# First attention with content and spatial head halves in three packed projections, with its last two blocks and the next stage's first gates in a new order

## What is computed

```python
q = (x @ Wq + bq) ...   # 2 heads of 64 features; k the same
q_content, q_spatial = (q[..., :half], q[..., half:])      # half = 32
q_spatial = _nrope(q_spatial...)                           # x1*cos - x2*sin, x1*sin + x2*cos
q = jnp.concatenate([q_content, q_spatial], axis=-1)       # k the same
score = jnp.einsum('bhqd,bhkd->bhqk', q, k) / sqrt(64)
attn = softmax(score); out = einsum('bhqk,bhkd->bhqd', attn, v)
return out.transpose(...).reshape(B, T, E) @ Wo + bo
```

## Time and profile before

| | |
|---|---|
| median of 3 runs | 709.2 us (709.16 to 710.09) |
| profiled execution, its own time | 709.26 us |
| span of the profiled execution | 707.5 us |
| mean granted clock of TensorE | 0.986 |
| first attention | from 0 to about 139 us of the span |
| busy over the span | TensorE 92%, VectorE 70%, ScalarE 64%, GpSimd 60% |

### The profile page before, as it was taken

One profiled execution on the slowest core, in us unless ns is written; L12 is line 12 of the kernel. 1 busy time (PEld: TensorE's weight loads), 2 busy tenths in 40 slices (PEclk: granted clock), 3 DMA queues, 4 the chain that ended last, 5 costly groups with the idle time before them and its releaser, 6 DMA issues.

```text
span 707.5 us, 14026 instructions
## 1 busy us (share of the span) xinstructions
PE 652.9 (92%) x4713; PEld 455.8 (64%) x4716; DVE 498.2 (70%) x958; ACT 450.7 (64%) x801; POOL 425.5 (60%) x443
## 2 busy tenths in 40 slices
PE   3789998799999999997999999998989999999997
PEld 1455555477777877675555555555546777787785
DVE  6879998676556778466778888877678565776521
ACT  3678886546665566545676677776765565666664
POOL 4545543368778777533346645654666877778673
PEclk9999999899999999998999999999999999999999
DMA  6101230000000000560467666664221000000001
GB/s 197 41 22 42 54 42 1 1 0 2 1 0 0 0 1 1 188 229 3 138 198 241 198 224 216 224 220 151 84 87 35 0 16 15 15 0 16 16 15 31
DMA packets 33028, 52.47 MB, mean 74 GB/s; under 512 B 4560, under 2 KB 9680, under 8 KB 32976
## 3 DMA queue, kind: packets, MB, share of 16 engines
q1 hardware_dynamic: 32784, 51.53, 23.3%
q10 hardware_dynamic: 192, 0.26, 0.1%
HBM read 27.15 MB, written 24.38 MB: 73 GB/s over the span
## 4 chain that ended last, share of the span: by engine, by line
PE 64%; DVE 16%; ACT 8%; issue 7%; DMA 2%; POOL 2%; DVEq 1%; ACTq 0%; POOLq 0%
PE banks L220 61%; ACT b_prob L1525 4%; DVE xn L182 3%; DVE a_mx L652 2%; ACT a_prob L553 2%; PE banks L212 1%; DVE f_gate L1088 1%; DVE f_h_hi L1091 1%; DVE a_prob L666 1%; DVE f_hidden L1094 1%; PE banks L977 1%; DVE a_straight L637 1%; DVE w_stage L857 1%; ACT f_g_hi L1044 1%; DVE stats L171 1%
## 5 line engine op out<-in xcount | busy, mean ns | idle before, releaser
L1158 POOL TENSOR_TENSOR f_g_lo<-f_gelu,f_g_hi 128x512 fp32r<-128x512 f32 x127 | 162.9, 1292 | 54.1 <-ACT f_g_hi L1044 53.6
L1043 ACT ACTIVATE f_gelu<-banks,cols 128x512 f32<-128x512 f32 x128 | 88.3, 690 | 132.5 <-PE banks L220 110.6
L1624 DVE TENSOR_REDUCE b_segment_max<-banks 128x6 f32<-128x768 f32 x128 | 120.0, 950 | 27.6 <-PE banks L220 27.0
L1741 POOL TENSOR_SCALAR_AFFINE_SELECT b_prob<-b_prob 128x512 f32<-128x512 f32 x128 | 81.7, 639 | 89.2 <-ACT b_prob L1525 88.5
L220 PE MATMUL banks<-f_g_hi,whi 128*128 128x512 f32 x320 | 130.2, 407 | 1.9 <-POOL f_g_lo L1158 1.4
L220 PE MATMUL banks<-f_g_lo,whi 128*128 128x512 f32 x320 | 126.7, 396 | 0.0
L1525 ACT ACTIVATE b_prob<-banks 128x768 f32<-128x768 f32 x128 | 102.4, 807 | 37.5 <-PE banks L220 37.2
L1151 POOL TENSOR_TENSOR f_h_lo<-f_hidden,f_h_hi 128x512 fp32r<-128x512 f32 x60 | 77.6, 1294 | 61.2 <-DVE f_hidden L1094 58.5
L220 PE MATMUL banks<-f_h_hi,whi 128*128 128x512 f32 x256 | 105.2, 411 | 6.2 <-POOL f_h_lo L1151 3.4
L220 PE MATMUL banks<-f_h_lo,whi 128*128 128x512 f32 x256 | 102.0, 398 | 0.0
L1044 ACT ACTIVATE f_g_hi<-banks,cols 128x512 fp32r<-128x512 f32 x128 | 87.4, 683 | 0.0
(11 more groups left out here) (125 smaller groups left out, 1096.4 us busy)
## 6 DMA issues: line engine op xcount, KB each, us to landing
f_h_hi<-b_q_dram SPq DMA_DIRECT2D x16, 512.0 KB, 4.1
f_h_lo<-b_k_dram SPq DMA_DIRECT2D x16, 512.0 KB, 5.2
b_o_dram<-b_o SPq DMA_DIRECT2D x8, 1024.0 KB, 4.4
b_q_dram<-b_q_hi SPq DMA_DIRECT2D x16, 256.0 KB, 3.3
b_k_dram<-b_k_hi SPq DMA_DIRECT2D x16, 256.0 KB, 3.0
w_stage<-in_wF SPq DMA_DIRECT2D x8, 352.0 KB, 3.2
b_q_dram<-b_q_lo SPq DMA_DIRECT2D x8, 256.0 KB, 3.4
b_k_dram<-b_k_lo SPq DMA_DIRECT2D x8, 256.0 KB, 3.1
```

The source lines that it names most:

```text
L1043: nc.scalar.activation(gf[c % 2][:, :], z_bank[c % 2], ACT.Gelu, scale=scale).then_inc(s_gf, 1)
L1158: nc.gpsimd.tensor_tensor(lo[:, c, :], gf[c % 2][:, :], hi[:, c, :].bitcast(F32), ALU.subtract).then_inc(s_glo[c % 2], 1)
L1624: nc.vector.reduce_max(seg[:, g, s, 2 * p:2 * p + 2, :], first_pass[:, 2 * p:2 * p + 2, 0:3 * P].rearrange("p b (c k) -> p b c k", c=3), A ...
L1741: nc.gpsimd.affine_select(out=pr, in_=pr, compare_op=ALU.is_ge, fill=0.0, base=0, pattern=[[0, 4], [1, P]], channel_multiplier=-1).then_in ...
```

## The change

- Wq and Wk become three packed 128x128 weights. `W_CONTENT` holds the 32 content features of q and k for both heads (4 x 32 rows out), `W_SPATIAL` the spatial ones, `W_SWAPPED` the same with the two groups of 16 swapped. Three projections a block stand for four.
- Content needs no rotation: ScalarE scales it and adds its bias (`act_content`). The spatial rows are rotated by two instructions on VectorE and one add on GpSimd. Then four transfers of SyncE a block (`sp_moves`) bring 64 rows each into the even and odd rows of qT and kT. The features of a head stand in another order, in q and k alike.
- The scale 1/8 is in q, and the maximum is written negated by the reduction itself.
- Probabilities are not divided. `pe_out` makes each head's output projection apart (8 products of contraction 64, into two banks), and `dve_update` adds each head times its inverse sum to x: 8 instructions of 128 columns for one of 512.
- The shift of the norm moves to GpSimd. The count of a weight piece on VectorE comes one body later, and a piece's load waits for GpSimd (`f_weights_lo`). The first two pieces move into body 0 on GpSimd and VectorE.
- Last block: `pe_gate` 0 stands ahead of `pe_pv` of sequence 0, the output of block 6 goes into the transposes' banks, and the transposes of sequence 1 wait until x of block 6 is updated. The next stage's second norm (`dve_apply(b1)`, `pe_T(SECOND_BLOCK)`) stands ahead of gate 3.

```diff
+            spatial_bank, misc, content_bank = banks[0:3]
...
+            def pe_content(pe, n):
+                wait(pe, s_co, n.t)
+                project(content_bank, wA[:, W_CONTENT, :], xnT[n.odd][:, :]).then_inc(s_wc, 1)
...
+            def pe_spatial(pe, n):
+                wait(pe, s_st, n.t)
+                project(spatial_bank, wA[:, W_SPATIAL, :], xnT[n.odd][:, :]).then_inc(s_ws, 1)
...
                 if s == 0:
-                    pe.wait_ge(s_ro, 2 * (b.t + 1))
+                    pe.wait_ge(s_mc, 16 * MOVES * (b.t + 1))
+                    pe.wait_ge(s_ms, 16 * MOVES * (b.t + 1))
...
-                pe.wait_ge(s_no[h], SEQS * b.t + s + 1)
+                pe.wait_ge(s_ex, UNITS * b.t + HA * s + h + 1)
...
-            def pe_out(pe, b, bank=y_bank):
+            def pe_out(pe, b, bank0=content_bank, bank1=spatial_bank):
                 pe.wait_ge(s_oc, b.t + 1)
-                token_major(bank, oT, wA[:, WO, :]).then_inc(s_y, 1)
...
+                for s in range(TILES):
+                    for h, bank in enumerate((bank0, bank1)):
+                        at = slice(DA * h, DA * (h + 1))
+                        last = mm(bank[:, s * P:(s + 1) * P], oT[at, s * P:(s + 1) * P], wA[at, WO, :])
+                last.then_inc(s_y, 1)
...
                 if before:
-                    pe_out(pe, b.after(-1))
+                    pe.wait_ge(s_co, b.t + 2)
+                    pe.wait_ge(s_st, b.t + 2)
+                    if two:
+                        pe_out(pe, b.after(-1))
+                    else:
+                        pe.wait_ge(s_vr, BLOCKS)
+                        pe_out(pe, b.after(-1), content_bank, misc)
...
                 if two:
-                    pe_proj(pe, n2, "qr")
-                    pe_proj(pe, n2, "q")
+                    pe_swapped(pe, n2)
+                    if before:
+                        pe.wait_ge(s_half, b.t)
+                    pe_content(pe, n2)
+                    if before:
+                        pe.wait_ge(s_done, b.t)
+                    pe_spatial(pe, n2)
...
-            def pe_last(pe, parts):
-                nxt = link["next"]
+                nxt["pe_gate"](pe, FIRST_BLOCK, 0, parts)
                 pe_pv(pe, LAST_BLOCK, 0)
-                pe.wait_ge(s_done, BLOCKS - 1)
-                nxt["pe_gate"](pe, FIRST_BLOCK, 0, parts)
+                pe_out(pe, LAST_BLOCK.after(-1), pT_bank[0], pT_bank[1])
                 pe.wait_ge(s_ex, UNITS * BLOCKS)
                 nxt["pe_gate"](pe, FIRST_BLOCK, 1, parts)
-                for h in (0, 1):
+                pe.wait_ge(s_done, BLOCKS - 1)
+                for h in range(HA):
                     pe_probT(pe, LAST_BLOCK, 1, h)
-                nxt["pe_T"](pe, SECOND_BLOCK)
                 nxt["pe_gate"](pe, FIRST_BLOCK, 2, parts)
                 pe_pv(pe, LAST_BLOCK, 1)
+                nxt["pe_T"](pe, SECOND_BLOCK)
                 nxt["pe_gate"](pe, FIRST_BLOCK, 3, parts)
             def pe_tail(pe, at, c):
                 if (at, c) == ("first", 0):
-                    pe_out(pe, LAST_BLOCK, o_bank)
+                    pe.wait_ge(link["next"]["split_written"], 2)
+                    pe_out(pe, LAST_BLOCK, o_bank, spatial_bank)
...
+            def act_content(act, n):
+                act.wait_ge(s_wc, n.t + 1)
+                wait(act, s_mc, 16 * MOVES * n.t)
+                nc.scalar.activation(content[:, :], content_bank[:, :], ACT.Identity, bias=b_content[:, :],
+                                     scale=col("factor")).then_inc(s_co, 1)
...
-                                                    bias=nm[s][:, h, qt:qt + 1], scale=SCALE_A,
-                                                    accum_out=total[s][:, h, qt:qt + 1])
+                                                    bias=nm[s][:, h, qt:qt + 1],
+                                                    accum_out=total[b.odd][:, s, h, qt:qt + 1])
...
+                wait(dve, s_ex, UNITS * (b.t - 1) + HA * (s + 1))
+                nc.vector.reduce_max(nm[s][:, :, :], score[:, :, :].rearrange("p h (q k) -> p h q k", q=2),
+                                     AX.X, negate=True).then_inc(s_nm, 1)
...
+            def dve_inverse(dve, b):
+                dve.wait_ge(s_ex, UNITS * (b.t + 1))
+                nc.vector.reciprocal(inv[b.odd][:, :, :, :], total[b.odd][:, :, :, :]).then_inc(s_in_, 1)
...
+            def dve_update(dve, b, h, bank):
                 dve.wait_ge(s_y, b.t + 1)
-                dve.wait_ge(s_bo, b.t + 1)
-                nc.vector.tensor_tensor(xblk(b.t), tiles_of(bank), xblk(b.t), ALU.add).then_inc(s_done, 1)
+                dve.wait_ge(s_in_, b.t + 1)
+                dve.wait_ge(s_half if h else s_bo, b.t + 1)
+                for s in range(TILES):
+                    x = X[:, bass.ds(TILES * b.t + s, 1), :]
+                    last = nc.vector.scalar_tensor_tensor(
+                        out=x, in0=tiles_of(bank)[:, s:s + 1, :], scalar=inv[b.odd][:, s // 2, h, s % 2:s % 2 + 1],
+                        in1=x, op0=ALU.mult, op1=ALU.add)
+                last.then_inc(s_done if h else s_half, 1)
...
                 dve_max(dve, LAST_BLOCK, 1)
-                dve_negate(dve, LAST_BLOCK, 1)
                 nxt["norm"].dve_stats(dve, b1)
-                dve_update(dve, LAST_BLOCK.after(-1))
-                dve_inverse(dve, LAST_BLOCK, 1)
-                dve_normalise(dve, LAST_BLOCK, 1)
+                dve_inverse(dve, LAST_BLOCK.after(-1))
+                nxt["dve_gate"](dve, b0, 0)
+                for h in range(HA):
+                    dve_update(dve, LAST_BLOCK.after(-1), h, pT_bank[h])
+                nxt["dve_gate"](dve, b0, 1)
+                nxt["dve_gate"](dve, b0, 2)
                 nxt["norm"].dve_apply(dve, b1, False)
-                for c in range(KC):
-                    nxt["dve_gate"](dve, b0, c)
-                    if c == 0:
-                        nxt["dve_xlo"](dve, b1)
+                nxt["dve_gate"](dve, b0, 3)
+                nxt["dve_xlo"](dve, b1)
             def dve_tail(dve, c):
                 if c == 0:
-                    dve_update(dve, LAST_BLOCK, o_bank)
-            def pool_rope(pool, n, k):
-                pool.wait_ge(s_st, 2 * n.t + k + 1)
-                pool.wait_ge(s_tu, 2 * n.t + k + 1)
-                nc.gpsimd.tensor_tensor((kT if k else qT)[n.odd][:, :], straight[:, :], turned[:, :],
-                                        ALU.add).then_inc(s_ro, 1)
+                    dve_inverse(dve, LAST_BLOCK)
+                    dve_update(dve, LAST_BLOCK, 0, o_bank)
+                    dve_update(dve, LAST_BLOCK, 1, spatial_bank)
...
+            def pool_rope(pool, n):
+                pool.wait_ge(s_st, n.t + 1)
+                pool.wait_ge(s_tu, n.t + 1)
+                wait(pool, s_ms, 16 * MOVES * n.t)
+                nc.gpsimd.tensor_tensor(spatial[:, :], straight[:, :], turned[:, :], ALU.add).then_inc(s_ro, 1)
...
+            def sp_moves(sp, n):
+                t = n.t
+                wait(sp, s_sc, SEQS * (t - 1))
+                sp.wait_ge(s_co, t + 1)
+                for i, to in enumerate((qT, kT)):
+                    sp.dma_start(to[n.odd][0:P:2, :], content[HALF_P * i:HALF_P * (i + 1), :]).then_inc(s_mc, 16)
+                sp.wait_ge(s_ro, t + 1)
+                for i, to in enumerate((qT, kT)):
+                    sp.dma_start(to[n.odd][1:P:2, :], spatial[HALF_P * i:HALF_P * (i + 1), :]).then_inc(s_ms, 16)
```

328 lines of the change are left out of this document (146 added, 182 removed).

## The result

The changed kernel takes 704.96 us (median of 17 runs, 702.03 to 708.86) against 709.17 (17 runs, 707.23 to 710.37). The ratio is 0.9944, 95% interval 0.9931 to 0.9956: faster by 4.2 us, half of the 8.5 that I forecast, and inside the range. Single executions scatter, though: two further profiles of the kernel before took 706.90 and 707.77 us.

A forecast was written before the change was run, and what follows sets the result against it. TensorE and VectorE were taken as full in the first attention's bodies. Gains 0.2 + 1.3 + 3.8 + 5.0 + 2.7 less 4.2 and 0.3 make 8.5 us: 709.3 to 700.8 us, range 694.5 to 707.5.

The forecast's parts named there:

- rival A: Output projection, bodies 1 to 6: its two heads don't run side by side, 6.4 us more, giving 707.2; chance 0.13.
- rival D: VectorE's eight updates at 0.5 us or more make it the bound; at 0.6 the time is 704.6; chance 0.03.
- rival B: Transfers land late, costing what a landing has above 3.7 us in 7 bodies; at 5.2, 711.3 us; chance 0.10.
- The stall in body 1: TensorE's 2.73 us wait for a late divided probability goes; body 1 takes 12.9 instead of 16.73, 3.8 us gained.
- the low clock near 42 us: First attention: TensorE's clock was forecast not to fall near 42 us any more; no separate size given.
- A steady body: Bodies 2 to 5 of the first attention: 11.9 us each instead of 13.14, bound by TensorE, 5.0 us gained.
- the start: Before body 0: one more landing against one projection less, 0.2 us gained, between 2 lost and 2 gained.
- the last block: End of the first attention: 4.2 us more than 17.85, since xn's new place ahead of gate 3 lengthens the chain.
- body 6: First attention: no projections of the next block, ends with the exponentials near 11.1 us instead of 13.77, 2.7 us gained.
- what stands behind: Feed-forward network after the last block: block 7's update in 8 instructions, VectorE 1.5 us later, 0.3 us lost on TensorE.

## Why the prediction was right and wrong

**Right.** The heads of the output projection run side by side: 0.99 us where I took 1.07, so rival A is out. Its price of 1.07 stays untested, since the heads overlapped even when they were issued apart. The updates are 0.28 us each (1.13 for four; rival D). The transfers land in 2.2 to 2.4 us, below the 3.3 that I took at most, and no body from 1 on waits for one (rival B). Only the first scores and body 0 do, 2.65 and 1.07 us. The Trainium skill, DMA: Bandwidth & Descriptors (section Anatomy of one DMA), gave an estimate of 2.3, and the trace agrees, on SyncE's path too. The stall in body 1 and the low clock near 42 us are gone, body 1 took 12.85 for 12.9. Of these two only the stall mattered: in the profile of the kernel before with an unused tile the clock stayed up there, and body 1 took 16.73 us as well.

**Mis-sized, in the kernel's favour.** A steady body takes 11.38, not 11.9. I took TensorE's group prices from the earlier trace rows, start to start, and added 0.2 for what was left over. Values take 1.02 now instead of 1.15 and input transposes 0.49 instead of 0.66, while v takes 1.09 instead of 0.99, and nothing is left over. That suggests small waits in those prices, which no run separates. That is 2.0 us over four bodies.

**Wrong: the start.** "One landing more, 3.3 at most, against one projection less" was sized at +0.2 between 2 lost and 2 gained, and it was -2.0, at the bad end. I counted one issue of the queue (0.44), not four of 0.6 behind each other, and left out what TensorE's idle time does to its clock. Two queues give 0.4 us back; the order of TensorE's work gives none.

**Wrong: the last block.** This is the step that failed the forecast: -7.2 for -4.2. The mechanism was the one that I named: xn in the chain ahead of gate 3, TensorE idle before the transposes (3.93 us), VectorE's xn beside GpSimd at 2.08 us, the low clock over gate 3. Moving xn ahead gives 4.2 us of last block back. Missing was the low clock at the block's beginning, 108 to 115 us: scores, transposes and gate 0 take 5.6 us (108.53 to 114.14), where they take 3.0 in the profile in which the clock stayed up (109.57 to 112.60). The whole block takes 21.99 us there, and I had forecast 17.85 + 4.2 = 22.05. So in that profile the chain came out as it was counted, and the term that I put at nothing is the low clock at its head. Whether it is paid is partly luck of the execution: the clock fell there after 0.95 to 2.07 us of idle time in eleven of the thirteen profiles with the change, and stayed up in two, after 1.90 and 1.92. Idle time at the end of body 6 stands before it, 0.89 us for the sum behind the update, and 1.90, of which 0.95 are the load of the branch number.

**Wrong: body 6.** 2.7 forecast, 1.9 measured. I let it end with the exponentials. It ended with the load of the branch number, which I hadn't priced: in the kernel before it took 0.49 us while the exponentials were still running. SyncE's stores of constant rows, now late because the transfers stand ahead of them in its queue, made it 2.07 us. I had asked only who waits for the transfers, not what stands behind them.

**Wrong: what stands behind.** -0.3 forecast, -1.2 measured: 0.5 gained up to 372 us, in the feed-forward network's first block above all, and 1.7 lost later in unchanged code, cause open. The 0.5 can't be credited to the change. In the profile of the kernel before, the clock was low from 137.94 to 144.77 us, over dense hidden products; in its second profile it was low only from 139.78 to 143.19, and the 15.5 us that follow the fourth low part were 1.1 us shorter.

## What to carry to other kernels

When work in the middle gets shorter, look at both ends: what fills them is a serial chain, and there the issues of a queue add up (four at 0.6 us), while idle time of TensorE may be paid a second time at the low clock. Whether it is differs from one execution to the next, so one profile doesn't price it: look for a second profile of the same code at the other clock before a difference goes to an edit. When something is put into a queue, list what stands behind it in that queue, and what that will now run beside. And when a wait goes down to an engine that had long been done, look at the waiting engine's own queue first.

## What I had not expected

Loading one number into TensorE's queue takes 0.49 us with the DMA engines free (six traces) and 2.01 to 2.22 us beside the constant rows' stores, some 49 GB/s (ten traces). The Trainium skill, DMA: Bandwidth & Descriptors (section Latency and other measured facts), puts a floor of about 600 ns under it, which these 0.49 us are below. And two heads in the halves of the array need not be issued in pairs to overlap: apart, they cost 0.3 us a body, since the second head's products ran beside the end of the first head's and the start of the next group's.
